# Two-layer gated cross-attention: keys of the second head pair and the output projection are issued in the next block's first units

## What is computed

```python
def _L1_xattn_ref(hidden_states, encoder_hidden_states, Wq, Wk, Wv, Wo, bo):
    ...
    q = hidden_states @ Wq          # 16 heads of 64
    k = encoder_hidden_states @ Wk
    v = encoder_hidden_states @ Wv
    ...
    scores = jnp.einsum('bhsd,bhkd->bhsk', q, k) * scale
    probs = jax.nn.softmax(scores, axis=-1)
    out = jnp.einsum('bhsk,bhkd->bhsd', probs, v)
    out = out.transpose(0, 2, 1, 3).reshape(B, S, H * Dh)
    out = out @ Wo + bo
    return out
```

## Time and profile before

| | |
|---|---|
| median of 3 runs | 1248.66 us (1243.88 to 1249.73) |
| the profiled execution | 1246.95 us, its span 1245.1 us |
| PE busy | 1092.0 us, 88% of the span |
| DVE busy | 903.0 us, 73% |
| ACT busy | 677.9 us, 54% |
| POOL busy | 278.6 us, 22% |
| mean granted PE clock | 0.957 of 2.4 GHz |

### The profile page before, as it was taken

One profiled execution on the slowest core, in us unless ns is written; L12 is line 12 of the kernel. 1 busy time (PEld: TensorE's weight loads), 2 busy tenths in 40 slices (PEclk: granted clock), 3 DMA queues, 4 the chain that ended last, 5 costly groups with the idle time before them and its releaser, 6 DMA issues. The chain is left out here.

```text
span 1245.1 us, 20138 instructions
## 1 busy us (share of the span) xinstructions
PE 1092.0 (88%) x6824; PEld 957.0 (77%) x6824; DVE 903.0 (73%) x1517; ACT 677.9 (54%) x1237; POOL 278.6 (22%) x280
## 2 busy tenths in 40 slices
PE   1869986997599879898989989898989988999998
PEld 1758876886388668797878878797977867888887
DVE  6689848898823578796978778797969765555555
ACT  3567755773211367585866767585867522232222
POOL 5050005002612310403031110403020122434432
PEclk9899998999699989999999999999999978999999
DMA  4000000002101000000000010000000004334432
GB/s 151 1 5 1 1 1 1 1 1 96 44 11 44 1 1 2 1 1 23 16 1 1 2 36 2 1 1 18 10 1 1 1 26 108 105 105 118 110 101 76
DMA packets 18046, 38.20 MB, mean 31 GB/s; under 512 B 3776, under 2 KB 10048, under 8 KB 17440
## 3 DMA queue, kind: packets, MB, share of 16 engines
q1 hardware_dynamic: 17952, 37.01, 10.0%
HBM read 35.76 MB, written 1.25 MB: 30 GB/s over the span
## 5 line engine op out<-in xcount | busy, mean ns | idle before, releaser
L270 PE MATMUL PS<-R 128*128 128x512 f32 (+2 forms) x2728 | 639.4, 380 | 69.2 <-DVE R L1343 14.2
L270 PEld LDWEIGHTS PS<-R 128*128 128x128 f32 x2728 | 466.1, 199 | 151.4 <-issue 35.7
L1295 DVE TENSOR_TENSOR R<-PS,R 128x512 fp32r<-128x512 f32 x352 | 224.8, 682 | 44.0 <-ACT R L1028 42.6
L1028 ACT ACTIVATE R<-PS 128x512 fp32r<-128x512 f32 x352 | 190.9, 596 | 84.4 <-PE PS L610 84.0
L621 PE MATMUL PS<-R 128*128 128x256 f32 x1408 | 204.4, 291 | 20.1 <-DVE FB L1303 19.8
L1002 ACT ACTIVATE FA<-PS,nmax 128x1024 f32<-128x1024 f32 (+1 forms) x160 | 192.6, 1204 | 50.1 <-DVE nmax L1284 28.2
L621 PEld LDWEIGHTS PS<-R 128*128 128x128 f32 x1408 | 181.3, 192 | 29.2 <-issue 12.9
L610 PE MATMUL PS<-eye,FA 128*128 128x128 f32 x1408 | 188.6, 278 | 14.4 <-ACT FA L1002 5.0
L610 PEld LDWEIGHTS PS<-eye,FA 128*128 128x128 f32 x1408 | 163.5, 143 | 45.3 <-issue 12.1
L1284 DVE TENSOR_REDUCE nmax<-PS 128x1 f32<-128x1024 f32 x128 | 155.7, 1222 | 15.0 <-PE PS L270 7.5
L424 POOL TENSOR_SCALAR R<-R 64x512 fp32r<-64x512 f32 x40 | 26.2, 655 | 406.4 <-ACT R L1145 346.5
(11 more groups left out here) (159 smaller groups left out, 1027.1 us busy)
## 6 DMA issues: line engine op xcount, KB each, us to landing
FB<-comb SPq DMA_DIRECT2D x48, 256.0 KB, 3.8
wst<-we_in SPq DMA_DIRECT2D x26, 384.0 KB, 4.0
wst<-w_in SPq DMA_DIRECT2D x4, 1024.0 KB, 5.6
wst<-w_in SPq DMA_DIRECT2D x3, 512.0 KB, 6.4
x<-x_in SPq DMA_DIRECT2D x2, 512.0 KB, 5.8
FB<-ctxT_in SPq DMA_DIRECT2D x2, 512.0 KB, 4.6
FB<-k_in SPq DMA_DIRECT2D x8, 128.0 KB, 2.5
FB<-ctxT_in SPq DMA_DIRECT2D x4, 256.0 KB, 4.0
```

Of the source, the lines that this page charges most:

```text
L270: last = mm(out, a, b, start=(n == 0), stop=(n == len(passes) - 1), skip_group_check=skip)
L1028: a_(L.pt[0][:, (u // 2) % 2, 4 * g_:4 * g_ + 4, (u % 2) * P:(u % 2) * P + P], L.turn(u, g_).rearrange("p (t n) -> p t n", t=4), ACT.Copy) ...
L1295: inc(v.tensor_tensor(lo, turned, hi.bitcast(F32), ALU.subtract), "p_lo")
```

## The change

The eight blocks are now written as one function `block(C, b, ...)` on each engine. Block 2 stands ahead of the loop, the loop holds an odd and an even block (3 and 4, 5 and 6, 7 and 8), block 9 stands behind it. The loop's end so lies after an even block.

The order and the PSUM banks of the 14 jobs change (`NEXT_ORDER`, `NEXT_BANKS`; `NEXT_FREED` says for which low part a job waits to reuse its bank). The two jobs for keys of head pair 1 come last, both in bank 5, and run in units 0 and 1 of the block that needs them; the second waits until ACT has copied the first. `out_project` of the block before runs in units 3 and 5, half each, in bank 5 too. `out_norm` is no longer ahead of the last jobs' place, and `spread_sums` comes one unit later, into FB instead of FA. In units 14 and 15 the jobs stand behind `values`, not ahead of it. In block 9 the statistics of the following normalization move from units 1, 2 and 4 to units 7, 8 and 10.

```diff
-PROJ_BANKS = [0, 1, 3, 4, 0, 1, 3, 4, 2, 5, 3, 4, 2, 5]
+NEXT_ORDER = [0, 2, 3, 1, 6, 7, 8, 9, 10, 11, 12, 13, 4, 5]
+NEXT_BANKS = [0, 1, 3, 4, 6, 3, 4, 6, 7, 3, 4, 6, 5, 5]
+NEXT_FREED = [0, 0, 0, 0, 0, 3, 4, 5, 0, 6, 7, 8, 0, 0]
...
+        def block(C, b, wo=None, wq=None, late=True, more=True):
+            J1 = 14 * (C - 1)
+            def fill(u):
+                if late and u in (0, 1):
+                    if u == 0:
+                        pe.wait_ge(s["at_norm"], 2 * C)
+                    else:
+                        pe.wait_ge(s["pj_hi"], J1 - 1)
+                    project(b, J1 - 14, range(12 + u, 13 + u))
+                if late and u in (3, 5):
+                    w = u // 2 - 1
+                    if w == 0:
+                        pe.wait_ge(s["pj_hi"], J1)
...
+                    out_project(L1, 1 - b, C - 1, (w,), (5, 5))
+                if more and u == UNITS - 2:
...
+                    project(1 - b, J1, range(1))
+                elif more and u == UNITS - 1:
+                    project(1 - b, J1, range(1, 4))
+            attention(L1, b, C, fill)
...
+            project(1 - b, J1, range(4, 6))
+            first_scores(C + 1, J1, 0)
+            out_rows(L1, C)
+            project(1 - b, J1, range(6, 8))
+            pe.wait_ge(s["o_sum"], BLOCKS * C + BLOCKS)
+            project(1 - b, J1, range(8, 12))
+            first_scores(C + 1, J1, 1)
...
-        with pe.Fori(0, NG1 - 1) as g_:
-            heads(g_, True)
-        heads(NG1 - 1, False)
+        block(2, 0, late=False)
+        with pe.Fori(0, NG1 - 1) as i:
+            block(2 * i + 3, 1, wo=i + 1, wq=i + 2)
+            block(2 * i + 4, 0)
+        block(2 * NG1 + 1, 1, wo=NG1, more=False)
...
+                if late and u in (1, 2):
+                    project_hi(C, J1 - 14, range(11 + u, 12 + u))
+                if more:
+                    project_hi(C + 1, J1, {UNITS - 2: range(1), UNITS: range(1, 2), UNITS + 1: range(2, 4)}.get(u, ()))
...
+            project_hi(C + 1, J1, range(4, 6))
+            exp(L1, C + 1, 0)
+            project_hi(C + 1, J1, range(6, 9))
+            out_hi(L1, b, C)
+            project_hi(C + 1, J1, range(9, 12))
...
+                if late and u in (4, 6):
+                    out_add(L1, 1 - b, C - 1, (u // 2 - 2,), (5, 5))
+                if more:
+                    project_lo(J1, {UNITS: range(2), UNITS + 1: range(2, 4)}.get(u, ()))
...
+            project_lo(J1, range(4, 5))
+            maximum(L1, C + 1, 0)
+            out_norm(L1, C)
+            project_lo(J1, range(5, 9))
+            out_lo(L1, b, C)
+            project_lo(J1, range(9, 12))
```

More of the change, by code:

```diff
@@ L670, in out_rows, with out_project @@
                     c = 512 * p + P * qt
-                    last = mm(PS[:, 2 + 3 * p, qt * P:qt * P + P], FA[:, c:c + P], eye_ap, start=True, stop=True)
+                    last = mm(PS[:, 2 + 3 * p, qt * P:qt * P + P], L.spread[:, c:c + P], eye_ap, start=True, stop=True)
                 last.then_inc(s["rbc"], 1)
-        def out_project(L, b, C):
+        def out_project(L, b, C, parts=range(2), banks=(6, 7)):
             pe.wait_ge(s["at_lo"], 2 * C + 2)
-            for w in range(2):
+            for w in parts:
                 for e in range(2):
@@ L767, in _ @@
                 context_turn(1, 0)
-            out_rows(b)
+            out_rows(L0, b)
             if b == 0:
@@ L820, in _, with project @@
             ffn3(base + c, c // 2, c % 2)
-        def project(b, J0, jobs, order=range(14), banks=PROJ_BANKS):
+        def project(b, J0, jobs, order=NEXT_ORDER, banks=NEXT_BANKS, freed=NEXT_FREED):
             for n in jobs:
                 j = order[n]
-                if n >= 4:
-                    pe.wait_ge(s["pj_lo"], J0 + n - 3)
+                if freed[n]:
+                    pe.wait_ge(s["pj_lo"], J0 + freed[n])
                 out = PS[:, banks[n], :]
@@ L1135, in _, with project_hi @@
                 a_(hf[:, c % 2, :], PS[:, c, :], ACT.Relu, scale=tg[:, 5:6]).then_inc(s["f_act"], 1)
-        def project_hi(C, J0, jobs, order=range(14), banks=PROJ_BANKS):
+        def project_hi(C, J0, jobs, order=NEXT_ORDER, banks=NEXT_BANKS):
             for n in jobs:
@@ L1186, in _ @@
         ln_split(2 * NB + 2, 1, LNH, SPARE_BANKS)
-        with act.Fori(0, NG1 - 1) as g_:
-            heads(g_, True)
-        heads(NG1 - 1, False)
+        block(2, 0, late=False)
+        with act.Fori(0, NG1 - 1) as i:
+            block(2 * i + 3, 1)
+            block(2 * i + 4, 0)
+        block(2 * NG1 + 1, 1, more=False)
         def job(j, c):
@@ L1495, in x_update, with project_lo @@
             return last
-        def project_lo(J0, jobs, order=range(14), banks=PROJ_BANKS):
+        def project_lo(J0, jobs, order=NEXT_ORDER, banks=NEXT_BANKS):
             for n in jobs:
@@ L1574, in _ @@
         dve.wait_ge(s["bo_added"], 2 * NB)
-        with dve.Fori(0, NG1 - 1) as g_:
-            heads(g_, True)
-        heads(NG1 - 1, False)
+        block(2, 0, late=False)
+        with dve.Fori(0, NG1 - 1) as i:
+            block(2 * i + 3, 1)
+            block(2 * i + 4, 0)
+        block(2 * NG1 + 1, 1, more=False)
         def job(j, c, comb_seen):
```

186 lines of the change are left out of this document (81 added, 105 removed).

## The result

| | before | after |
|---|---|---|
| median | 1247.24 us (8 runs, 1243.88 to 1249.73) | 1254.58 us (8 runs, 1250.86 to 1256.58) |
| the profiled execution, its span | 1246.95, 1245.1 us | 1255.51, 1253.7 us |
| mean granted PE clock | 0.957 | 0.947 |
| ratio | | 1.0063, 95% interval [1.0042, 1.0084] |

The forecast was 1244.1 with 1236 to 1253; the time lies above it. Of 8.6 us between the two spans, 0.9 has come by the turn of unit 14 in block 2 (488.47 and 489.36), 6.1 comes from there to the same turn of block 8, 1.4 from there to the router's products (the first of the mixture of experts), and 0.2 behind them.

What follows compares the result with a forecast made beforehand. PE sets the pace, DVE 3% behind. Seven boundaries to unit 6 took 336.7 us; after, 7 x 46.1 plus loop's end 2 x 1.5 plus clock 4 x 1.6 gives 332.1: gain 4.6, median 1244.1, range 1236 to 1253.

Steps and rivals of the forecast that it cites:

- The clean boundary: Undisturbed block boundary, turn of unit 14 to turn of unit 6: 46.1 us after against 45.9 before, no gain.
- The walk's three waits: PE idle in each boundary: 1.2 us ahead of `out_rows`, 1.0 ahead of scores of unit 1, 2.6 for ACT's keys copy.
- its cover: `out_add` in DVE's busy units, 2 x 0.75 us, covered by PE's wait; without that cover up to 1.5 each block.
- The splits: POOL's weight splits move to units 4 to 7 of odd blocks, away from `out_lo`: 3 x 1.26 = 3.8 us saved.
- The loop's end: At two boundaries DVE's jump of 2.4 us delays the maximum of unit 1: +1.5 us each, against 2.2 before.
- my rivals: Clock holds (0.24), falls at every boundary (0.12), keys-copy wait paid more than once (0.12), POOL's splits hold DVE (0.04).
- the slower one: Units 1 to 4: wait for ACT's keys copies paid more than once, 1.6 us each further time, 1260; chance 0.12.
- a loop's end of more than 2.4: Sign that the prediction is wrong: a loop's end taking more than 2.4 us.
- The clock: PE's granted clock falls at four of seven boundaries, at 1.6 us each, with the new 2.6 us wait.
- replaced: In the clean boundary, vanishing waits (1.9, 1.1 to 2.4, 0.8 us) are replaced by 1.2 + 1.0 + 2.6.

Runs made afterwards that it cites:

- e6: The changed kernel with the loop taken away on PE alone, DVE and ACT keeping theirs: 1241.6 us, 0.9973 of the kernel before.
- e7: The changed kernel with the loop taken away on DVE and ACT, kept on PE: 1253.4 us, 1.0078 of the kernel before.
- e14: The changed kernel with ACT's copies of the first late keys job one unit earlier and no loop on PE: 1217.8 us, 0.9784 of the kernel before.
- e11: The kernel before with the loop's end moved after even blocks, and no loop on PE: 1256.3 us, 1.0093 of the kernel before.
- e13: The kernel before with the loop's end moved after even blocks, and no loop on DVE and ACT: 1245.2 us, 0.9992 of the kernel before.
- e4: The changed kernel with ACT's copies of the first late keys job in unit 0 instead of unit 1: 1229.4 us, 0.9881 of the kernel before.
- e1: The changed kernel with its blocks written out without loops on PE, ACT and DVE: 1239.5 us, 0.9944 of the kernel before.
- e8: The changed kernel with the output projection's 24 products back in the boundary, ahead of scores of unit 1: 1245.5 us, 1.0 of the kernel before.
- e9: The changed kernel with PE's scores of unit 1 moved to the start of the next loop iteration: 1252.9 us, 1.0059 of the kernel before.

## Why the prediction was wrong

**The clean boundary was right.** "46.1 against 45.9": 47.36 with a fall, less 1.5, is 45.9, and the clean period is 67.3 in both kernels. The walk's three waits, 1.2, 1.0 and 2.6, came as 0.85, 1.20 and 2.38, each with the releaser it named; their sum was 0.4 too high. In the stretches inside a block nothing moved (2.76 for a unit); `out_add` took 0.74 there and had its cover.

**The splits were right.** `out_lo` takes 1.30 at 646.02, and POOL holds nobody: under L526 DVE's maximum took what it takes elsewhere, the order of the row being POOL's split and DVE's maximum beside it:

```profile
530.96 3.52 POOL L526 TENSOR_TENSOR R<-wst,R 128x1536 fp32r<-128x1536 f32 x1
```

```profile
533.00 1.22 DVE L1306 TENSOR_REDUCE nmax<-PS 128x1 f32<-128x1024 f32 x1
```

**The loop's end was mis-sized, and this is the failed step.** "the jump's 2.4 brings the maximum of unit 1 to 24.0 instead of 22.4 ...: +1.5 each". I let DVE's gap alone stand for it. The two periods are 6.8 and 8.4 over the clean one; with one fall of 1.5 in the first and two in the second that leaves 5.3 and 5.4, together 10.7 against 3.0 (a fall behind a loop's end is taken at the price of the others). The cause is PE's own gap, which e6 and e7 show. For DVE's gap by itself 1.5 was about right: 1.2 to 1.5 a period in e6 and e14, where PE has no loop. PE's gap was missing from the sum. It could be seen in the trace of before, in a row that I had read as a part of DVE's 2.2:

```profile
588.71 1.18 PE L270 MATMUL PS<-R 128*128 128x512 f32 x4 [1.66 <-issue]
```

What I did not ask was what covered it: the 24 products of `out_project` between PE's last wait and the loop's end. The change takes these away, and its text hides that, since the loop is not what it edits there. The part that a gap of DVE plays was not wrong in general (e11, e13), but it was not the one in this order. None of my rivals had the loop's end in it; the slower one spoke of repeated waits in units 1 to 4, and those were not there. Of the signs of being wrong, "a loop's end of more than 2.4" is the one that came.

**The clock fell seven times at the boundaries, not four**, at 1.5 us where I had priced 1.6: 10.6 us against 6.4. Five of these falls follow the new wait of 2.4 us, as the prediction has it, only more often; the two others follow the loop's ends, where it had none.

Together 10.7 + 10.6 = 21.3 against 3.0 + 6.4 = 9.4, so 11.9 of the 13.1 us between the forecast for the profiled execution (1242.4) and its time (1255.5). The rest is small. The clean boundary is 0.2 shorter than my walk, 1.4 less in seven. A fall in block 9 that the prediction did not have (0.52 at 970, behind a wait of 1.94 for DVE) adds 1.4: e4 without it takes 1.4 less there. The 0.9 ahead of block 2's end and the 0.2 behind the router are what single executions differ by anyway (487.1 to 490.9 for that turn in the variants of the new order).

**What I had called "replaced" was a choice.** I set the new wait of 2.6 against the old waits and found nothing gained. The sum was right, but the wait was only ACT's order: e4 shows 3.4 us for each boundary behind it. A forecast of no change with a wait of 2.6 in it is also a statement on what is still to be had.

## What to carry to other kernels

Before moving work away from the end of a hardware loop, count on each engine what is queued between its last wait and the loop's end: here PE stood idle for 3.5 to 4.3 us with 1.2 us of work queued there, and for 1.1 to 1.7 with 4.1 us. Two surcharges that were paid in different boundaries cost 1.8 us more a pair here when they came to lie in the same one. A wait for a short copy is worth a look at what stands ahead of it in its engine's queue: two operations moved behind it were worth 3.4 us a boundary here.

## What the runs showed of the hardware

**Around a loop's end more instructions are transferred.** The profile counts the transfers of instructions by queue. After, 640 to 656 us, with the loop's end:

```profile
q8 instruction: 3, 0.05, 1.4%
q14 instruction: 5, 0.04, 0.9%
```

In the same 16 us of a boundary without a loop's end (576 to 592) there is one transfer. In e1, at the place of the former loop's end, there are two:

```profile
q8 instruction: 1, 0.02, 0.5%
q14 instruction: 1, 0.01, 0.2%
```

The Trainium skill says why ("Runtime: NRT & Kernel Launch", Instruction fetch mechanics): instructions are prefetched in sequence, and a taken branch to a target outside the window that is held makes the engine wait for a transfer of it. The traces agree, with eight transfers against one or two; without PE's loop there are six (e6), without DVE's and ACT's four (e7). Beside them stand idle times of 1.1 to 4.2 us on PE and 2.2 to 2.5 us on DVE. That these transfers are what PE waits for is the page's word; the traces show both at the same place. The other page of the Trainium skill that the prediction used ("Advanced Engine Details and Errata", Control Flow Timing) has 108 ns for a compare-and-branch; the idle time here is ten times that and more.

**There can be a second gap.** PE had 1.0 to 1.7 us more of it after one transpose of eight, in after, e4 and e7, where little was queued, and none in before, e8 and e9.

**The clock fell after most waits of 2.4 us in after, and after none of 1.2 us in e14.** In after it was near 0.50 behind five of seven waits of 2.4 us and behind both loop's ends. In e14, where PE's waits from 505 to 900 us were 1.2 at most, it never fell. Between these lengths before has it both ways: 0.50 from 501 us on, behind a wait of 1.86, and no fall behind the 1.86 at 569.50.
